# First layer's attention scores in 128x32 column tiles, with the causal limit as 32 further contracted rows

## The reference, cut to what matters

```python
kv = latent @ Wkv_up
k, v = (kv[..., :HEAD_DIM], kv[..., HEAD_DIM:])      # one key and one value head of 8, shared
att = jnp.einsum('bthd,bsd->bhts', q, k) * scale     # 16 heads, 512 x 512
att = jnp.where(causal[None, None], att, -jnp.inf)
att = jax.nn.softmax(att, axis=-1)
y = jnp.einsum('bhts,bsd->bthd', att, v)
```

## Time and profile before

| what | before |
|---|---|
| median of 3 runs | 949.93 us (944.2 to 950.81) |
| the profiled execution | 942.1 us, its span 940.3 us |
| PE busy | 780.7 us, 83% |
| VectorE, ScalarE, GpSimd busy | 568.2, 447.0, 408.4 us |
| mean granted clock of TensorE | 0.907 |
| the costliest groups of this attention | L817 191.3 us, L595 158.3, L415 125.2, L369 99.3, L394 87.4 us |

### The profile page before, as it was taken

How to read it: one execution, slowest core, us unless ns; L and a number is a source line. 1 busy time by engine, 2 the same in 40 slices (tenths; PEclk the granted TensorE clock), 3 DMA queues, 4 the chain that set the end, 5 groups by cost and what they waited for, 6 DMA issues and landing times.

```text
span 940.3 us, 21506 instructions
## 1 busy us (share of the span) xinstructions
PE 780.7 (83%) x8454; PEld 380.5 (40%) x8454; DVE 568.2 (60%) x1509; ACT 447.0 (48%) x726; POOL 408.4 (43%) x533
## 2 busy tenths in 40 slices
PE   4586979798889898897688999977876788999887
PEld 2232323333333333333334444443434345666555
DVE  3875747576757575626577333420348858888884
ACT  1001645455545455563332433423334868888664
POOL 6221012233232232031001688888754659886433
PEclk9655999999989999998798998987995989999999
DMA  5311253236433332131300233333330011111101
GB/s 130 72 46 33 67 151 79 67 86 166 97 66 81 81 88 75 31 96 36 113 0 10 51 43 41 44 44 44 31 53 12 9 25 26 24 36 23 26 26 34
DMA packets 72122, 53.20 MB, mean 57 GB/s; under 512 B 23608, under 2 KB 65024, under 8 KB 71424
## 3 DMA queue, kind: packets, MB, share of 16 engines
q1 hardware_dynamic: 62168, 44.28, 18.6%
q0 software_dynamic: 9856, 7.58, 6.1%
HBM read 31.76 MB, written 18.23 MB: 53 GB/s over the span
## 4 chain that ended last, share of the span: by engine, by line
PE 49%; DVE 17%; POOL 10%; DMA 9%; issue 7%; ACT 3%; SPq 3%; POOLq 1%; DVEq 0%; ACTq 0%
PE bank L415 7%; PE ps_s L369 7%; PE bank L394 6%; POOL d_acc L1316 5%; DVE MX L817 4%; PE ps_o L1520 4%; POOL XG L1306 3%; PE b1ps L2010 3%; PE b1ps L2021 3%; PE ps_s L378 2%; DVE R L1412 2%; DMA Q<-d_q 2%; PE b1ps L2034 2%; DMA d_m<-ms 2%; DMA Q<-d_m 1%
## 5 line engine op out<-in xcount | busy, mean ns | idle before, releaser
L817 DVE TENSOR_REDUCE MX<-bank 128x1 f32<-128x320 f32 (+13 forms) x352 | 191.3, 566 | 102.9 <-PE bank L422 99.2
L595 ACT ACTIVATE PR<-ps_s 128x1024 f32<-128x1024 f32 x160 | 158.3, 1023 | 156.7 <-PE ps_s L378 90.7
L415 PE MATMUL bank<-K,Q 96*32 96x32 bf16 (+15 forms) x2048 | 125.2, 308 | 41.6 <-DVE MX L817 21.8
L369 PE MATMUL ps_s<-Q,K 99*128 99x512 bf16 x320 | 99.3, 400 | 5.6 <-DMA Q<-d_m 5.6
L415 PEld LDWEIGHTS bank<-K,Q 96*32 96x32 bf16 x2048 | 44.5, 99 | 146.5 <-DVE MX L817 75.9
L1316 POOL DMA_INDIRECT d_acc<-Y,idx x56 | 87.6, 1565 | 20.8 <-issue 15.9
L1520 PE MATMUL ps_o<-H,w 128*128 128x512 f32 x176 | 90.3, 664 | 0.0
L1306 POOL DMA_INDIRECT XG<-d_tab,idx x56 | 54.0, 965 | 79.1 <-DVE idx L1421 62.6
L394 PE MATMUL bank<-PR,VE 128*32 128x512 f32 x640 | 87.4, 623 | 0.0
L1640 ACT ACTIVATE H<-ps_h,b1T 128x512 f32<-128x512 f32 x88 | 60.4, 687 | 42.3 <-PE ps_h L1508 39.9
L944 POOL TENSOR_SCALAR ve<-mv 128x4 f32<-128x4 f32 x8 | 1.9, 234 | 177.6 <-DVE mv L682 177.6
(11 more groups left out here) (347 smaller groups left out, 1391.8 us busy)
## 6 DMA issues: line engine op xcount, KB each, us to landing
Q<-d_q SPq DMA_DIRECT2D x24, 384.0 KB
d_q<-qs SPq DMA_DIRECT2D x24, 128.0 KB, 2.4
X<-L_attn_x SPq DMA_DIRECT2D x8, 256.0 KB, 4.7
w<-L_ffn_W SPq DMA_DIRECT2D x8, 256.0 KB, 4.3
d_acc<-zrow SPq DMA_DIRECT2D x1, 2048.0 KB, 10.1
w<-L_ffn_W SPq DMA_DIRECT2D x1, 2048.0 KB, 10.0
AC<-d_acc SPq DMA_DIRECT2D x8, 256.0 KB, 3.0
d_y<-ysb SPq DMA_DIRECT2D x112, 18.0 KB
```

Of the source, the lines that this page charges most:

```text
L369: last = nc.tensor.matmul(ps_s[half][:, 512 * hh:512 * hh + 512], K[b % QB][0:KM, P * i:P * i + P], Q[b % QB][0:KM, 4 * hg:4 * hg + 4, P * ...
L415: nc.tensor.matmul(ps_mx[G % 2][o:o + QW, x * w:(x + 1) * w], Q[b % QB][0:KR, 4 * c + hh, QW * j:QW * j + QW], K[b % QB][0:KR, 0:w], start ...
L595: nc.scalar.activation(PR[t % 2][:, 2 * half:2 * half + 2, :], ps_s[half][:, :].rearrange("p (a f) -> p a f", a=2), ACT.Exp, scale=DH ** - ...
L817: nc.vector.tensor_reduce(MX[b % 2][:, c:c + len(cs)], ps_mx[G % 2][:, 0:len(cs) * w].rearrange("p (x w) -> p x w", w=w), AX_X, ALU.max).t ...
```

## The change

The scores of a half are computed as eight products of 32 keys by 512 columns, in 128x32 column tiles. The 512 columns are now 32 queries of all 16 heads, so that a half is 64 queries of 16 heads instead of 128 queries of 8 heads; each of four tiles holds 32 of the 128 keys. In a diagonal step the block where keys and queries have the same 32 positions contracts 32 more rows, which hold the causal limit (`KC`, `QC`, sent into rows 75 to 106 of every `K` and `Q` by six DMAs at the start). Blocks wholly above the diagonal are filled with -1e30 by a product that contracts a single row; in the built program this product's tile is 32x32, while that of the others is 128x32. The products with `maskT` and `maskX` go away, and so do the clearing of `Q` and `K` and the zero rows: 75 rows are contracted instead of 99, and 72 instead of 96 in the maxima. The exp of a half writes into 32-element pieces of `PR`.

```diff
-KR = 96
-KM = KR + PARTS
+KM = NPR + PARTS
+QW = 32
+KQ = KM + QW
...
-            for hh in range(2):
-                hg = 2 * half + hh
-                last = nc.tensor.matmul(ps_s[half][:, 512 * hh:512 * hh + 512], K[b % QB][0:KM, P * i:P * i + P],
-                                        Q[b % QB][0:KM, 4 * hg:4 * hg + 4, P * g:P * g + P],
-                                        start=True, stop=(i < g), skip_group_check=(i == g))
-            if i == g:
-                for c in range(2):
-                    part = ps_s[half][:, 512 * c:512 * c + 512].rearrange("p (h q) -> p h q", q=P)
-                    eye = bc(identb[64 * c:64 * c + 64, 64 * c:64 * c + 64].unsqueeze(1), [64, 4, 64])
-                    for turn in range(2):
-                        o = 64 * (c ^ turn)
-                        last = nc.tensor.matmul(part[:, :, o:o + 64], (maskT, maskX)[turn][64 * c:64 * c + 64, :], eye,
-                                                start=False, stop=(turn == 1), tile_position=(64 * c, 0),
-                                                skip_group_check=True)
+            q_, k_ = Q[b % QB], K[b % QB]
+            for c in range(2):
+                j = 2 * half + c
+                for kt in range(NT):
+                    o = QW * kt
+                    out_ = ps_s[half][o:o + QW, 512 * c:512 * c + 512]
+                    if i == g and kt > j:
+                        last = nc.tensor.matmul(out_, maskT[0:1, QW:2 * QW], bc(identb[0:1, 0:1], [1, 512]),
+                                                start=True, stop=True, tile_position=(0, o))
+                    else:
+                        r = KQ if i == g and kt == j else KM
+                        last = nc.tensor.matmul(out_, k_[0:r, P * i + o:P * i + o + QW],
+                                                q_[0:r, :, P * g + QW * j:P * g + QW * j + QW],
+                                                start=True, stop=True, tile_position=(0, o))
...
-                    if b == 0:
-                        for q in Q[1:]:
-                            clear(q).then_inc(s_qz, 1)
...
+                if n == -1 and s == 0:
+                    sp.wait_ge(s_eye, 1)
+                    for i in range(QB):
+                        sp.dma_start(K[i][NPR:KQ, :], KC[:, :]).then_inc(s_kc, 16)
+                        sp.dma_start(Q[i][KM:KQ, :, :], bc(QC[:, :].unsqueeze(1), [QW, NH, T])).then_inc(s_kc, 16)
```

## The result

The changed kernel is slower. Its median is 979.96 us (974.97 to 980.54, four runs) against 948.62 us (944.2 to 950.81, four runs) for the kernel before: a ratio of 1.033, with a 95% interval of 1.0294 to 1.0366.

What follows compares the result with a forecast made beforehand. The prediction took SyncE's queue to pace each batch's second part and VectorE's reductions step 1. Its terms, -2.1 - 0.2 - 1.2 + 0 = -3.5 us, took 949.9 to 946.4 us, with a range of 933 to 957.

Steps and rivals of the forecast that it cites:

- the products: Score steps: a diagonal step takes 2.11 us, 0.17 more than before; an off-diagonal step gains 0.38 us.
- below full packing: Rival, column tiles in the scores: a 512-column round takes 1.26 times as long; 956 us in all; chance 0.04.
- slower: Rival, score products: the moving operand in 64-byte pieces reads at half pace, +42 us, 992 us; chance 0.08.
- No drain at the fills: Rival, diagonal steps: fills and key products overlap, a step takes 0.90 us; -24 us, 926 us; chance 0.10.
- the queue: Batches' second part: SyncE's transfers end 27.7 us after rc however fast PE runs, so later steps' gains become waits.
- more gets through than the queue allows: Rival, steps 4 to 8: their gains count too because loads come earlier; -15 us, 935 us; chance 0.12.
- 2 to 3 us a batch: End of batches: PE's waits for the loads Q<-d_m and Q<-d_q grow to this size.
- 2 to 3 us for stretches at half clock that fall otherwise: Whole kernel: the clock's allowance within the forecast's own range of 940 to 952 us.
- Costed at nothing. The 24 fewer contracted rows.: Scores and maxima: contracting fewer rows keeps the same pace per column, so it was costed at nothing.
- the start: Before the first maxima: without GpSimd's clearing VectorE's cast ends 2.16 us earlier; taken as -2.1 us.
- They go out behind that load: Start: six new transfers, 1.68 MB, follow the load of Q and delay nothing, needed only at 80 us.
- That rival: Start: the six transfers share engines with the load of Q, delaying it up to 9 us; up to 956 us; chance 0.06.

Runs made afterwards that it cites:

- fill75: Changed kernel with the fills contracting 75 rows instead of one, so every product is in 128x32 tiles: 934.21 us, ratio 0.9845 to the kernel before.
- pad_late: Changed kernel; fills contract 128 rows, key products 96 off the diagonal, 128 on it; added rows sent as 48 and 5 after Q's first load: 928.81 us, ratio 0.9812.
- fill32: Changed kernel with the fills contracting 32 rows instead of one, their tile staying 32x32: 964.02 us, ratio 1.0165 to the kernel before.
- before_max72: Kernel before with one edit, the maxima contracting 72 rows instead of 96: 952.87 us, ratio 1.0072.
- old_both: Changed kernel with old score products and masks in both kinds of steps, keeping 75 and 72 rows and the new start: 959.98 us, ratio 1.0025.
- old_diag: Changed kernel with old score products and masks back in the diagonal steps alone: 962.85 us, ratio 1.0067 to the kernel before.
- fill128: Changed kernel with the fills contracting 128 rows instead of one: 936.67 us, ratio 0.9809 to the kernel before.
- fill_late: Changed kernel with fills contracting 128 rows and the six transfers sent only after the first load of Q has landed: 934.27 us, ratio 0.988.

## Why the prediction was wrong

**Right: the products.** A diagonal half was forecast at 1.25 and 0.86 us and takes 1.27 and 0.86 at full clock; the off-diagonal half, 0.45, takes 0.43. Each change between 128x32 and 32x32 tiles costs 0.10 us, for runs of 0.213 us start 0.30 to 0.33 apart. Column tiles run fully side by side, so the rival "below full packing" falls: 1024 columns for each of four tiles in 0.43 us. The moving operand in pieces of 64 bytes costs nothing, so the rival "slower" named the right side by luck, with a wrong cause. "No drain at the fills" falls too. Its diagonal step of 0.90 us is what `fill75` shows (0.44 + 0.43), where there is no drain, but its 926 us knew nothing of the clock: `fill75` measures 934.2, `pad_late` 928.8. ScalarE's exp takes 1023 ns in both kernels, whatever pieces it writes.

**Right: the queue.** From `d_r` to the next batch in batch 5 there were 27.7 us; after, from the issue at 365.82 to PE at 393.77, there are 27.95, with the same order of transfers:

```profile
365.82 0.35 SPq L1045 DMA_DIRECT2D d_r<-rc  x1
...
389.83 0.83 SPq L1099 DMA_DIRECT2D Q<-d_m  x3
```

```profile
393.77 0.39 PE L380 MATMUL ps_s<-Q,K 107*32 107x512 bf16 x1 [0.65 <-DMA Q<-d_m]
```

That is why the loss of batch 5 stands ahead of `rc`, 24.92 us for 17.84, and not behind it, 28.92 us for 28.64. `pad_late` tests the same with faster steps: there `rc` of batch 5 comes 17.03 us after the start of the batch, and from `d_r` (324.50) to the next batch (351.78) are 27.28 us. Nothing speaks for the rival "more gets through than the queue allows". The waits for `Q<-d_m` between 82 and 440 us grew from 5.6 to 7.7 us in all, not to 2 to 3 us a batch. That PE had less time to give at half clock fits this, and in `fill75` they are 9.3 us, but it was not tested by itself.

**Wrong, the larger part: "2 to 3 us for stretches at half clock that fall otherwise".** This was the range's whole provision for the clock. The sum took the fills and their serial runs for their time at full clock alone, and left the clock as it was in the earlier trace rows, which had been chosen for being at 1.00. The runs show 134 us at half clock instead of 32.

What does such time cost at the end? Between kernels whose work at full clock is alike it can be read off. From `fill32` to the changed kernel there are 49 us more of it in the traces and 17.1 us more attention; over the runs (from mean clock and span) 41 us more, and some 16 us of time. From the kernel before to `before_max72` the runs show 15 us more, and 7 us of time. So a third to a half of it reaches the end. As an estimate from that, the roughly 100 us added here cost 33 to 50 us, and the attention lost 37.9 in the traces. The clock is enough to explain the loss; these figures can't divide it more finely.

By parts, with the ratios, each against the kernel before timed beside it, the kernels are slower by: fewer rows alone (`old_both`) 0.25% (-0.2 to 0.7), the new products with their serial runs on top (`fill32`) 1.65%, the single row on top of that (the changed kernel) 3.3%. Of the 31.3 us between the medians that is about 2, 13 and 16 us. The 16 us of the single row are shown. The middle part is not resolved: at full clock the products take the forecast time, and the traces show 85 us at half clock for 62 in `old_both`, but why the clock is lower there, and lower still in `old_diag`, was not separated. The parts do not simply add either: `fill75` has the new products too, and a faster attention than the kernel before at 0.90.

**Wrong, the smaller part: "Costed at nothing. The 24 fewer contracted rows."** The step looked only at the pace per column, which indeed stays. It did not ask what the rows do to the granted clock. `before_max72` has that edit for the maxima alone and is 0.7% slower (0.4 to 1.1), with a mean clock of 0.894 for 0.901. For both kinds of product together `old_both` can't be told from no cost.

**Half right: the start.** VectorE's cast takes 0.23 us without GpSimd's clearing beside it, and the load of `Q` goes out 2 us earlier, as forecast. "They go out behind that load" failed: transfers issued later ran beside it. That rival had 0.06, with a forecast of up to 7 us later; what happened lies between (0.2 us later), and the start gained nothing.

## What to carry to other kernels

A product that is cheap in time can be dear in clock. Before shrinking what TensorE contracts, or adding products with one row, try the edit alone and read the granted clock of the stretch, not only whether PE is busy. Compare clocks over several executions: two of the same attention differed by up to 18 us at half clock here. Where products of different size are to run side by side, give them one tiling, if need be by contracting zeros: here that edit of one line turned 3.3% slower into 1.5 to 1.9% faster. And a transfer whose number of rows is a prime above 16, as 53 here, should be cut into parts whose numbers of rows have larger divisors.

## What the runs showed of the hardware

- PE was busy for 19.89 of 20.50 us with the clock at half throughout, in batch 5 of the changed kernel. Fills of 32 rows in the place of one row, with the same starts at full clock, left 85 us at half clock instead of 134, and a kernel 1.65% slower than before instead of 3.3%.
- The same attention had 79 and 61 us at half clock in two executions (`fill128`, `fill_late`).
- Rows of zeros count for the granted clock: with 24 fewer of them in the maxima of the kernel before its mean over the runs went from 0.901 to 0.894, with 29 more in the scores to 0.910.
- Changing between a 128x32 and a 32x32 tiling costs 0.09 to 0.12 us a time (0.30 to 0.33 us from start to start of a run of 512 columns), whether one row is contracted or 32.
- A transfer of 53 rows moved 24 to 26 GB/s, one engine's share; SyncE stood for 35 us in each of the issues behind it. The same bytes as 48 and 5 rows did not delay the first exp.
- Transfers issued behind a load on the same queue slow it while it runs: 1.7 us of 9.5 for 1.68 MB behind 1.15.
